# Scores kept scaled up to the exponential, and four pieces of scalar and low-half work put on GpSimd

## The reference

```python
h = jnp.maximum(_layernorm(x, axis=-1), 0.0)
x = x + _L0_gnn_ref(h, adj, Wq, bq, Wk, bk, Wv, bv, Wo, bo)
h = jnp.maximum(_layernorm(x, axis=-1), 0.0)
x = x + _L1_gnn_ref(h, adj, weight, wq, wk)
```

## Time and profile before

| | |
|---|---|
| median of 3 runs | 1935.76 us (1935.14 to 1937.50) |
| profiled execution, its own time | 1939.41 us |
| its span, first to last instruction | 1937.6 us |
| TensorE products / weight loads busy | 93% / 72% |
| VectorE, ScalarE, GpSimd busy | 84%, 57%, 23% |
| mean granted TensorE clock | 0.987 of full |
| DMA | 142.5 MB moved, 74 GB/s |
| chain that ended last | TensorE 49%, VectorE 30%, issue 8%, DMA 6%, ScalarE 3% |

### The profile page before, as it was taken

One profiled execution on the slowest core, in us unless ns is written; L12 is line 12 of the kernel. 1 busy time (PEld: TensorE's weight loads), 2 busy tenths in 40 slices (PEclk: granted clock), 3 DMA queues, 4 the chain that ended last, 5 costly groups with the idle time before them and its releaser, 6 DMA issues.

```text
span 1937.6 us, 53466 instructions
## 1 busy us (share of the span) xinstructions
PE 1798.5 (93%) x16817; PEld 1395.1 (72%) x16817; DVE 1625.1 (84%) x4904; ACT 1111.1 (57%) x2381; POOL 453.1 (23%) x1190
## 2 busy tenths in 40 slices
PE   3689999999999999999999999999999999999986
PEld 2457777777777777777777777777777777777763
DVE  5688888888888888888888888888888888888883
ACT  2356555666656565656556565656666555556551
POOL 1022221222122122212222222212221221222111
PEclk9889999999999999999999999999999999999997
DMA  3412122222212222222222221222222122222111
GB/s 107 138 52 75 51 84 79 83 67 78 78 52 81 81 71 77 78 68 65 79 84 67 77 78 52 81 78 84 67 78 77 51 81 81 70 77 78 53 45 38
DMA packets 195401, 142.48 MB, mean 74 GB/s; under 512 B 36000, under 2 KB 167072, under 8 KB 195360
## 3 DMA queue, kind: packets, MB, share of 16 engines
q1 hardware_dynamic: 178224, 108.93, 19.7%
q10 hardware_dynamic: 17136, 33.03, 5.5%
HBM read 57.94 MB, written 16.78 MB: 39 GB/s over the span
## 4 chain that ended last, share of the span: by engine, by line
PE 49%; DVE 30%; issue 8%; DMA 6%; ACT 3%; SPq 2%; ACTq 1%; DVEq 1%; POOL 0%; POOLq 0%
PE ring L360 36%; DVE probs_t_lo L800 6%; DVE probs L792 6%; PE turned L425 4%; DMA out_dram<-x 3%; PE pv L443 2%; PE score L410 2%; PE ring L478 2%; DMA stack<-stage 2%; DVE work L859 2%; DVE x L930 1%; SPq L318 1%; DVE o_sum L813 1%; DVE x L906 1%; DVE val L891 1%
## 5 line engine op out<-in xcount | busy, mean ns | idle before, releaser
L588 ACT ACTIVATE probs<-probs,least 128x256 f32<-128x256 f32 x1024 | 461.9, 500 | 181.7 <-DVE least L792 152.1
L792 DVE CUSTOM_DVE_ANT_0 probs<-score,far,undo_score 128x256 f32<-128x256 f32 x1024 | 451.3, 478 | 34.2 <-PE score L410 18.6
L1081 POOL TENSOR_TENSOR heads_out<-o_sum,o_rcp 128x64 f32<-128x64 f32 x512 | 145.3, 305 | 1149.2 <-DVE o_sum L813 1139.9
L800 DVE TENSOR_TENSOR probs_t_lo<-turned,probs_t_hi 128x512 f16<-128x512 f32 x512 | 350.1, 684 | 7.3 <-ACT probs_t_hi L598 7.3
L598 ACT ACTIVATE probs_t_hi<-turned 128x512 f16<-128x512 f32 x512 | 301.0, 588 | 78.0 <-PE turned L425 78.0
L425 PE MATMUL turned<-ident,probs 128*128 128x128 f32 x2048 | 310.9, 275 | 20.5 <-ACT probs L588 20.5
L425 PEld LDWEIGHTS turned<-ident,probs 128*128 128x128 f32 x2048 | 244.8, 142 | 66.1 <-ACT probs L588 30.0
L443 PE MATMUL pv<-val,probs_t_hi 128*128 128x65 f16 x2048 | 185.4, 192 | 36.6 <-DVE probs_t_lo L800 35.1
L410 PE MATMUL score<-stack 128*128 128x256 f16 x1024 | 196.6, 274 | 19.7 <-DMA stack<-stage 19.5
L443 PEld LDWEIGHTS pv<-val,probs_t_hi 128*128 128x128 f16 x2048 | 152.2, 97 | 70.9 <-DVE probs_t_lo L800 45.7
L445 PE MATMUL pv<-val,probs_t_lo 128*128 128x33 f16 x2048 | 178.2, 179 | 0.0
(11 more groups left out here) (160 smaller groups left out, 4309.7 us busy)
## 6 DMA issues: line engine op xcount, KB each, us to landing
stack<-stage SPq DMA_DIRECT2D x2048, 32.0 KB, 1.9
x<-x_dram ACTq DMA_DIRECT2D x32, 512.0 KB, 4.4
out_dram<-x SPq DMA_DIRECT2D x32, 512.0 KB, 2.9
xa<-x_dram ACTq DMA_DIRECT2D x31, 512.0 KB, 3.6
adj_in<-adj_dram SPq DMA_DIRECT2D x32, 256.0 KB, 3.0
adjt_in<-adj_t_dram SPq DMA_DIRECT2D x32, 256.0 KB, 3.0
wq_raw<-wq_dram SPq DMA_DIRECT2D x2, 512.0 KB, 6.9
wk_raw<-wk_dram SPq DMA_DIRECT2D x2, 512.0 KB, 8.5
```

The lines of the kernel that those rows point to most:

```text
L588: last = nc.scalar.activation(probs[:, u % 2, q, :], probs[:, u % 2, q, :], ACT.Exp, bias=least[:, u % 2, q:q + 1], scale=-1.0)
L792: last = nc.vector.tensor_tensor_reduce(out=probs[:, u % 2, q, :], in0=score[u % 2][:, q * NODES:(q + 1) * NODES], in1=far[:, q, :], scale ...
L800: nc.vector.tensor_tensor(pL[:, u % 2, :, :], turned[u % 2][:].rearrange("p (k n) -> p k n", k=QT), pH[:, u % 2, :, :], ALU.subtract).then ...
L1081: last = nc.gpsimd.tensor_tensor(dst, o_sum[:, pair % 2, q:q + 3:2, :], o_rcp[:, pair % 2, q:q + 3:2].unsqueeze(2).broadcast_to([P, 2, HEAD]),
```

## The change

- L792 loses the scaling by `undo_score`: `probs` and `least` stay scaled. A new GpSimd operation for each head (`peaks`) writes `peak = least * undo_score`; ScalarE's exponentials take `peak` as bias and a per-partition scale `minus_undo` in place of the constant -1.
- The first layer norm's normalisation moves from VectorE to GpSimd (`first_normalise`), at the same step 12; GpSimd's Newton steps get one more (the mean with its sign turned) and are spread over steps 9, 10 and 11.
- In the second softmax, GpSimd scales the maximum (`l1_top`); the scaling of the sums goes; GpSimd multiplies the exponentials by `l1_rcp` and 2^13 in place, ScalarE copies them to `e_hi` in one operation, and GpSimd makes `e_lo` in one subtraction.
- The floor of the scale search goes from 2^-60 to 2^-40.

```diff
-NSTEPS = (3 + 4 * NEWTON_ROUNDS, 2 + 3 * NEWTON_ROUNDS)
+NSTEPS = (4 + 4 * NEWTON_ROUNDS, 2 + 3 * NEWTON_ROUNDS)
@@ ScalarE
-                act.wait_ge(masked, count(b, HEADS, u))
+                act.wait_ge(peaked, count(b, HEADS, u))
                 for q in range(QT):
                     last = nc.scalar.activation(probs[:, u % 2, q, :], probs[:, u % 2, q, :],
-                                                ACT.Exp, bias=least[:, u % 2, q:q + 1], scale=-1.0)
+                                                ACT.Exp, bias=peak[:, u % 2, q:q + 1],
+                                                scale=minus_undo[:, 0:1])
...
-                                                    bias=l1_max[:, m:m + 1], scale=undo[:, 5:6],
+                                                    bias=l1_top[:, m:m + 1], scale=undo[:, 5:6],
...
                 if s == AL_STEP + 2:
-                    act.wait_ge(l1_rcped, count(b, 1, 0))
+                    act.wait_ge(e_ok, count(b, 1, 0))
...
-                    for m in range(QT):
-                        last = nc.scalar.activation(eH[:, m, :], work[:, 1, m * NODES:(m + 1) * NODES],
-                                                    ACT.Copy, scale=l1_rcp[:, m:m + 1])
-                    last.then_inc(hi["e"], 1)
+                    nc.scalar.activation(eH[:].rearrange("p m n -> p (m n)"), work[:, 1, :],
+                                         ACT.Copy).then_inc(hi["e"], 1)
@@ VectorE
-                        in1=far[:, q, :], scale=undo_score[:, 0:1], scalar=FAR, op0=ALU.add, op1=ALU.min,
+                        in1=far[:, q, :], scale=1.0, scalar=FAR, op0=ALU.add, op1=ALU.min,
...
-                    dve.wait_ge(l1_maxed, count(b, 1, 0))
-                    nc.vector.tensor_scalar(l1_max[:], l1_max[:], undo[:, 5:6], None, ALU.mult
-                                            ).then_inc(l1_topped, 1)
                 if s == AL_STEP + 2:
                     dve.wait_ge(l1_exped, count(b, 1, 0))
-                    nc.vector.tensor_scalar(l1_sum[:], l1_sum[:], 1.0 / E_LIFT, None, ALU.mult
-                                            ).then_inc(l1_summed, 1)
-                    dve.wait_ge(l1_summed, count(b, 1, 0))
+                    settle(dve, dve_settled)
                     nc.vector.reciprocal(l1_rcp[:], l1_sum[:]).then_inc(l1_rcped, 1)
-                if s == AL_STEP + 3:
-                    dve.wait_ge(hi["e"], count(b, 1, 0))
-                    for m in range(QT):
-                        last = nc.vector.scalar_tensor_tensor(
-                            out=eL[:, m, :], in0=work[:, 1, m * NODES:(m + 1) * NODES],
-                            scalar=l1_rcp[:, m:m + 1], in1=eH[:, m, :],
-                            op0=ALU.mult, op1=ALU.subtract)
-                    last.then_inc(lo["e"], 1)
...
-                    if s == NORM1 and cur and later:
-                        normalise(0, xa, xa, n + 1)
@@ GpSimd
+            def first_normalise(b):
+                for q in range(QT):
+                    nc.gpsimd.tensor_scalar(xa[:, q, :], xa[:, q, :], minus_mean[:, q:q + 1],
+                                            rstd[0][:, q:q + 1], ALU.add, ALU.mult
+                                            ).then_inc(normed[0], 1)
+
+            def peaks(u, b):
+                pool.wait_ge(masked, count(b, HEADS, u))
...
+                settle(pool, pool_settled)
+                nc.gpsimd.tensor_scalar(peak[:, u % 2, :], least[:, u % 2, :], undo_score[:, 0:1],
+                                        None, ALU.mult).then_inc(peaked, 1)
+
+            def second_softmax(s, b):
+                if s == AL_STEP + 1:
+                    pool.wait_ge(l1_maxed, count(b, 1, 0))
+                    settle(pool, pool_settled)
+                    nc.gpsimd.tensor_scalar(l1_top[:], l1_max[:], undo[:, 5:6], None, ALU.mult
+                                            ).then_inc(l1_topped, 1)
+                if s == AL_STEP + 2:
+                    pool.wait_ge(l1_rcped, count(b, 1, 0))
+                    settle(pool, pool_settled)
+                    for m in range(QT):
+                        part = work[:, 1, m * NODES:(m + 1) * NODES]
+                        last = nc.gpsimd.tensor_scalar(part, part, l1_rcp[:, m:m + 1], E_LIFT,
+                                                       ALU.mult, ALU.mult)
+                    last.then_inc(e_ok, 1)
+                if s == AL_STEP + 3:
+                    pool.wait_ge(hi["e"], count(b, 1, 0))
+                    nc.gpsimd.tensor_tensor(eL[:].rearrange("p m n -> p (m n)"), work[:, 1, :],
+                                            eH[:].rearrange("p m n -> p (m n)"), ALU.subtract
+                                            ).then_inc(lo["e"], 1)
...
                 for s in range(HEADS):
-                    if s == VAR1 and later:
-                        reciprocal_deviation(n + 1)
+                    if prev:
+                        second_softmax(s, p)
                     if s == 0 and prev:
                         norm_heads(HEADS // 2 - 1, p)
                     elif s > 0 and s % 2 == 0 and cur:
                         norm_heads(s // 2 - 1, t)
+                    if cur and s + AHEAD < HEADS:
+                        peaks(s + AHEAD, t)
+                    elif nxt and s + AHEAD >= HEADS:
+                        peaks(s + AHEAD - HEADS, n)
+                    if s in (VAR1, VAR1 + 1, VAR1 + 2) and later:
+                        reciprocal_deviation(n + 1, s - VAR1)
+                    if s == NORM1 and later:
+                        first_normalise(n + 1)
```

More of the change, by code:

```diff
@@ L155, in two_layers @@
         undo_score = sb("undo_score", [P, 1], f32)
+        minus_undo = sb("minus_undo", [P, 1], f32)
         undo_out = sb("undo_out", [P, 1], f32)
@@ L176, in two_layers @@
         least = sb("least", [P, 2, QT], f32)
+        peak = sb("peak", [P, 2, QT], f32)
         pH = sb("probs_t_hi", [P, 2, QT, NODES], f16)
@@ L194, in two_layers @@
         l1_sum = sb("l1_sum", [P, QT], f32)
+        l1_top = sb("l1_top", [P, QT], f32)
         l1_rcp = sb("l1_rcp", [P, QT], f32)
@@ L199, in two_layers @@
         rstd = [sb(f"rstd{n}", [P, QT], f32) for n in (1, 2)]
+        minus_mean = sb("minus_mean", [P, QT], f32)
         newton = [sb(f"newton{n}", [P, 3, QT], f32) for n in (1, 2)]
@@ L736, in find_scale @@
                 step(nc.vector.tensor_reduce(most[:, 0:1], bank[:, 0:P], AX.X, ALU.max))
-                step(nc.vector.tensor_scalar(most[:, 1:2], most[:, 0:1], 2.0 ** -60, 2.0 ** 60,
+                step(nc.vector.tensor_scalar(most[:, 1:2], most[:, 0:1], 2.0 ** -40, 2.0 ** 60,
                                              ALU.max, ALU.min))
@@ L854, in reciprocal_deviation, with second_normalise @@
                                                         op0=ALU.add, op1=ALU.mult))
[L856 to L857 removed]
+            def second_normalise(b):
+                dve.wait_ge(nstep[1], count(b, NSTEPS[1], NSTEPS[1] - 1))
                 for q in range(QT):
[L859 to L861 removed]
+                    nc.vector.tensor_scalar(work[:, q, :], x1[:, q, :], meanvar[1][:, q, 0:1],
+                                            rstd[1][:, q:q + 1], ALU.subtract, ALU.mult
+                                            ).then_inc(normed[1], 1)
             def relu_low(dst, src, high, done):
@@ L961, in body @@
                     if prev and s == NORM2:
-                        normalise(1, x1, work, p)
+                        second_normalise(p)
                     if prev:
@@ L1005, in body @@
                             split_low(c)
-                if later and not cur:
-                    normalise(0, xa, xa, n + 1)
             for q in range(QT):
@@ L1029, in _ @@
             step(nc.vector.tensor_tensor(undo_score[:], undo[:, 0:1], undo[:, 1:2], ALU.mult))
+            step(nc.vector.tensor_scalar(minus_undo[:], undo_score[:], -1.0, None, ALU.mult))
             step(nc.vector.tensor_scalar(scale[:, 0:1], scale[:, 0:1], -SCALE, None, ALU.mult))
@@ L1034, in _ @@
             step(nc.vector.memset(tops[:], 0.0))
-            normalise(0, xa, xa, 0)
             for c in range(FIRST):
@@ L1047, in _, with reciprocal_deviation @@
                                     ).then_inc(ident_ok, 1)
-            def reciprocal_deviation(b):
+            def reciprocal_deviation(b, portion):
                 v, y = newton[0][:, 0, :], rstd[0][:]
                 a, c = newton[0][:, 1, :], newton[0][:, 2, :]
-                at = [0]
+                at = [4 + 4 * portion if portion else 0]
                 def step(ins):
@@ L1059, in step, with first_guess @@
                     at[0] += 1
-                pool.wait_ge(var_ok[0], count(b, 1, 0))
-                settle(pool, pool_settled)
+                if portion == 0:
+                    pool.wait_ge(var_ok[0], count(b, 1, 0))
+                    settle(pool, pool_settled)
+                    first_guess(step, v, a, y)
```

(13 more changed lines are left out.)

9 lines of the change are left out of this document (7 added, 2 removed).

## The result

The median goes from 1935.45 us (4 runs, 1934.01 to 1937.50) to 2007.17 us (4 runs, 2006.75 to 2008.38): 1.0371 times as long, 95% interval 1.0353 to 1.0389. The profiled execution took 2007.4 us, its span is 2005.6.

What follows compares the result with a forecast made beforehand. TensorE sets the pace, 53.2 of 57.01 us a graph. GpSimd's chain makes av0 3.8 us later, less 1.25 of VectorE relief: 2.55 us a graph, 74 us over 29 passes, so about 2012 us; range 1925 to 2060.

Steps and rivals of the forecast that it cites:

- the relief: TensorE's gaps outside the stretch before av0: a lighter VectorE saves 1.25 us a graph, between 0 and 2.9.
- The chain: GpSimd's in-order queue from the first Newton step to e_lo: 15.4 us, so av0 comes 3.8 us later.
- the four one-input operations: GpSimd's two normalisations and two scalings of the exponentials ahead of e_lo: 3.88 us together.
- the two-input slope: GpSimd's f32 two-input rows, 2.19 ns a column, taken as price for the normalisations and scalings.
- The sign named first: TensorE waits for GpSimd's e_lo subtraction, 2 to 4 us, in each of some 30 graphs.
- The recorded estimate from the page: The skill page's 1.8 cycles a column: the four operations about 3.0 us, the time about 1986.
- The turn of head 1: TensorE idles 0.6 us there behind VectorE's L930; 0.5 us of that gap go.
- The wait on the val half: TensorE's wait for VectorE's L891, 0.3 us each; 0.25 us a graph of it was taken as saved.
- The per-head peak: GpSimd's small operation after each mask delays exponentials 0.4 to 1.4 us; covered, so taken at nothing.
- The faster one: Low halves ready nearly in time, VectorE was the brake: about 1915 us; chance 0.17.
- The rate of L1119: Rival: GpSimd's one-input operations at L1119's rate, 6.3 us, av0 6.2 late, 2083 us; chance 0.10.
- That the mask's constant changes nothing: Rival: on VectorE, L792's scalar costs the same as the constant; relief halves, 2030 us; chance 0.07.

Runs made afterwards that it cites:

- e1: The changed kernel with the next graph's mask made on GpSimd at step 5 instead of step 10; 1947.5 us.
- e3: The changed kernel, same operations reordered on GpSimd: next graph's mask at step 5, Newton portions at steps 13 to 15, normalisation at the end of step 15; 1900.9 us.
- e9: The kernel before with only the scores' part (constant in mask, peaks, two-operand exponentials), Newton over steps 9 to 11, changed floor, next graph's mask at step 5; 1921.8 us.
- e7: e3 without the scores' part: mask and exponentials of the kernel before, no peaks on GpSimd; 1920.9 us.
- e10: The kernel before with the next graph's mask at step 5 and nothing else; 1947.5 us.
- e5: The kernel before with the constant 1.0 in place of undo_score in the mask, so the scores are not scaled back; 1918.1 us.
- e8: The kernel before with the exponentials' scale -1 read from a per-partition column instead of a constant; 1940.6 us.
- e11: e3 with four more GpSimd operations of 512 columns, results not used, at the end of step 15; 1971.4 us.

## Why the prediction came out right

Direction, mechanism and the time (2012 forecast, 2007 measured) hold, and e1 to e3 show the mechanism. That the time came out within 5 us is luck: the cost was forecast 0.8 us a graph too high and the relief 0.65 too high, and the two nearly cancel.

- **The chain.** Forecast: 15.4 us and av0 3.8 late. Measured: 14.6 from 939.33 to 953.92, av0 at 14.69, so 2.98 late against the earlier trace rows. The term that failed is the four one-input operations: 3.88 forecast by the two-input slope, 2.44 measured (1.51 and 0.93 in the timeline), which is outside the 3.0 to 5 us that the forecast of 1985 to 2045 assumed. The time fell in that range all the same, since the relief was smaller (below) and the rest of the chain is 12.2 us, not 11.5: the small operations with a per-partition scalar take 0.29 us, not 0.20 (Newton's, without one, 0.19), and three gaps of 0.40, 0.30 and 0.21 us stand in the chain, which I had taken as without any. The sign named first, a wait of 2 to 4 us before av0, came smaller: it is 1.18 us, and most of the rest stands before the turn of head 13 and the weighing, at 1.09 and 0.44.
- **The Trainium skill's rate,** GPSIMD Engine Reference, section Performance versus the Vector engine: 1.8 cycles a column is 0.77 us for 512 columns, and the row has 762 ns. It agrees. So the two-input slope was the wrong neighbour, and half of that slope, the cheap side of the forecast (2.2 us), was the near one. The recorded estimate from the page is not right either: at 0.77 us for 512 columns the four operations are 2.3 us, not 3.0, and the same sum then gives about 1965 us, not 1986. That is an estimate from the page. It has the price of these four nearly right and is still further from the truth than mine, through the rest of the chain and the next term.
- **The relief.** Forecast 1.25 us outside the stretch; measured 0.60 (44.07 to 43.47). L933 (L930 before) no longer starts late; VectorE itself waits there for TensorE in each pass (before: 4 times in the whole run):

```profile
DVE x L933 <- PE ring L364: 41.8, 32, 2.9
```

  The turn of head 1 waits 0.35 us on average in place of 0.57, where I had taken 0.5 off. The wait on the val half kept its size (0.3 us, 25 times in the middle of the run, as before). The burst on VectorE in front of it did shrink with its masks, from 2.32 to 2.19 us between the start of the second norm's normalisation and that of the val half in one graph of each trace; but TensorE comes to the wait 0.12 us sooner as well, counted from the same start.
- **The per-head peak.** Forecast: covered. e9 shows it. Inside the stretch the cover of head 12, said to just hold, is gone: its exponentials end 0.05 us before the turn, on average. The 1.4 us taken there left out the eight Newton steps, which also stand ahead of that peak: it starts 1.6 us after the row's minimum is ready.
- **The rivals.** The faster one had its deciding point at a lateness under the relief. Its condition is not met, 2.97 against 0.60, but e3 shows that the argument for it, VectorE as the brake, was sound: with the queue cleared, the same operations take 1900.9 us. The rate of L1119 is out (762 ns for 512 columns against 1084 for 256 from integers). That the mask's constant changes nothing is out (418 ns).

What stays open: how much of e7's 20 us over e3 is the effect of e10 and how much the scores' part (e5, e8 and e10 by themselves give 19 - 3 + 8 = 24, an estimate from their times); and why two of VectorE's operations stretch in e10, which was not tried by itself.

## What to carry to other kernels

Before work goes to an idle engine, list what that engine does, in order, between the input and the awaited result. Its idle share does not tell the cost: here 36% busy cost 72 us, 38% busy with the same operations in another order won 35, and more work still, at an idle place, cost none. Follow each awaited result also through the engines that stand between: e_hi was late on ScalarE only because a peak for another head was. Where no row has the price of a new operation, check the neighbour that is taken against the number of inputs as well as the type: here f32 with two inputs took 2.19 ns a column, integers with one input 4.2, and the operation itself, f32 with one input, 1.5.

## What the runs showed of the hardware

- A per-partition scalar in place of a constant costs 60 ns on VectorE's custom mask (478 and 418), 92 on a ScalarE exponential (500 and 592) and about 0.1 us on a small GpSimd operation (0.29 and 0.19). On a GpSimd operation of 512 columns, two of them cost 0.14 us (762 ns, and 620 with two constants in e11).
- GpSimd from f32: 762 ns for 512 columns with one input and two scalars, 1154 to 1269 with two inputs; from integers 1084 for 256.
- Two small VectorE operations stretched, 169 to 332 and 161 to as much as 400 ns, as GpSimd began operations of 1.07 us (e10, e7); others beside the same operations did not.
- In the pass of e11 that is shown, the granted clock fell to 1.2 GHz until about 952 us, after TensorE had been busy for 1.2 of the 3 us from 946 to 949. Passes with such a fall are 1.4 us longer than the others of that run. Its mean granted clock is 0.973, against 0.986 in e3.
